# Three PSUM banks each for two kinds of scores, and a maximum taken bank by bank, in the narrow attention of a four-layer cross-attention kernel

## What is computed

```
cq = heads(ci @ cq_w, NH, CHD)                # NH = 16, CHD = 8
ckv = encoder_outputs @ ckv_w                 # 1601 rows of context
ck, cv = jnp.split(ckv, 2, axis=-1)
ck, cv = (heads(ck, NH, CHD), heads(cv, NH, CHD))
cctx = sdpa(cq, ck, cv, causal=False)         # softmax(q k / sqrt(8)) v
hidden_states = hidden_states + cctx @ cdense_w
```

## Time and profile before

| | us |
|---|---|
| median of 3 runs (5559.66 to 5569.71) | 5564.36 |
| the profiled execution's own time | 5575.49 |
| its span | 5573.7 |
| narrow attention in it, from the first to the last score (L1295, L1308) | 2295.7 to 3211.3 |
| mean granted TensorE clock over the span | 0.947 |

### The profile page before, as it was taken

The page is one execution under the profiler, slowest core; times in us unless marked ns, Lnnn a source line. Parts: engine busy times, 40 slices in busy tenths (PEclk is TensorE's granted clock), DMA queues, the critical chain, the costliest instruction groups (busy, mean ns, idle before and its releaser), DMA issues. The chain is left out here.

```text
span 5573.7 us, 95075 instructions
## 1 busy us (share of the span) xinstructions
PE 4920.9 (88%) x31384; PEld 3667.6 (66%) x31384; DVE 3625.5 (65%) x5212; ACT 3238.2 (58%) x4943; POOL 2589.8 (46%) x1723
## 2 busy tenths in 40 slices
PE   6999999999997799699899969767999999999987
PEld 5777676777766577455555559545777677667766
DVE  5777777777774344567666646235777777777764
ACT  5676767676662455355555620336677676767662
POOL 3666666676661233111111132003666676666661
PEclk9999999999998899699999979887999999999998
DMA  1000000000000000222222200101000000000000
GB/s 51 7 1 8 7 1 7 7 1 7 1 1 16 25 0 0 44 41 41 41 45 38 28 32 0 74 30 35 7 1 7 7 1 7 7 7 1 1 1 30
DMA packets 35067, 93.58 MB, mean 17 GB/s; under 512 B 12896, under 2 KB 22368, under 8 KB 33504
## 3 DMA queue, kind: packets, MB, share of 16 engines
q1 hardware_dynamic: 34656, 88.47, 7.2%
HBM read 55.80 MB, written 2.10 MB: 10 GB/s over the span
## 5 line engine op out<-in xcount | busy, mean ns | idle before, releaser
L1028 ACT ACTIVATE L_attn_probs<-L_attn_ps_s,L_attn_bias_now 128x512 f32<-128x512 f32 x1664 | 1093.8, 688 | 312.0 <-PE L_attn_ps_s L776 284.7
L739 POOL TENSOR_TENSOR L_attn_sums<-L_attn_sums,L_attn_probs 128x1024 f32<-128x1024 f32 x512 | 1224.7, 2392 | 103.8 <-POOL L_attn_sums L739 80.7
L930 DVE TENSOR_TENSOR L_attn_ps_x<-L_attn_probs,L_attn_ps_x 128x512 f32<-128x512 f32 x1408 | 978.0, 695 | 259.8 <-ACT L_attn_probs L1028 209.8
L942 DVE TENSOR_TENSOR L_attn_probs<-L_attn_probs,L_attn_ps_x 128x3072 f32<-128x3072 f32 (+2 forms) x384 | 933.7, 2460 | 85.9 <-PE L_attn_ps_x L825 85.9
L1034 ACT ACTIVATE L_attn_probs<-L_attn_probs 128x3072 f32<-128x3072 f32 (+2 forms) x384 | 774.7, 2051 | 122.9 <-DVE L_attn_probs L942 121.2
L774 PE MATMUL L_attn_ps_s<-L_attn_g_hi,L_attn_ctx_hi 128*128 128x512 f32 x1664 | 730.9, 439 | 125.6 <-ACT L_attn_probs L1028 93.0
L812 PE MATMUL L_attn_ps_u<-L_attn_probs,L_attn_v_sb 128*64 128x256 f32 (+1 forms) x6656 | 776.9, 384 | 0.0
L1564 ACT ACTIVATE L_cross_probsT<-L_cross_ps_st 128x512 f32<-128x512 f32 (+1 forms) x832 | 491.3, 597 | 367.9 <-PE L_cross_ps_st L1308 338.6
L775 PE MATMUL L_attn_ps_s<-L_attn_g_lo,L_attn_ctx_hi 128*128 128x512 f32 x1664 | 668.6, 402 | 0.0
L776 PE MATMUL L_attn_ps_s<-L_attn_g_hi,L_attn_ctx_lo 128*128 128x512 f32 x1664 | 667.0, 401 | 0.0
L1446 DVE TENSOR_REDUCE L_cross_part<-L_cross_ps_s 128x1 f32<-128x804 f32 x512 | 498.2, 992 | 242.5 <-PE L_cross_ps_s L1295 236.5
(11 more groups left out here) (288 smaller groups left out, 9218.4 us busy)
## 6 DMA issues: line engine op xcount, KB each, us to landing
L_cross_kx<-A SPq DMA_DIRECT2D x256, 100.5 KB, 2.8
L_attn_ctx_in<-in_ctxT SPq DMA_DIRECT2D x16, 804.0 KB, 4.4
memory_ctx<-in_ctx SPq DMA_DIRECT2D x8, 832.0 KB, 6.0
Bw<-in_ctxT SPq DMA_DIRECT2D x8, 804.0 KB, 4.4
memory_ctxT<-in_ctxT SPq DMA_DIRECT2D x8, 804.0 KB, 4.4
A<-in_L_mlp_w SPq DMA_DIRECT2D x4, 1024.0 KB, 6.0
X<-in_x SPq DMA_DIRECT2D x1, 2048.0 KB, 8.5
L_norm_wq<-in_L_w_wq SPq DMA_DIRECT2D x2, 1024.0 KB, 7.6
```

Source lines behind the costliest of these rows:

```text
L739: pool.tensor_tensor(both, both, p[:, k:k + 2, :], ALU.add).then_inc(added_up, 1)
L930: dve.tensor_tensor(high[:, :] if k == KT - 1 else ps_x[:, :], tile, ps_x[:, :], ALU.max).then_inc(maxed, 1)
L942: dve.tensor_tensor(s, s, ps_x[:, :].unsqueeze(1).to_broadcast([P, count, W]), ALU.subtract).then_inc(shifted, 1)
L1028: act.activation(probs[j % 2][:, k, :], ps_s[(KT * j + k) % 4][:, :], ACT.Identity, bias=bias_now[:, k:k + 1]).then_inc(taken, 1)
```

## The change

The 8 banks are divided in another way: three banks for the scores of the maximum, used in turn by single matmuls, and three for the turned scores. DVE takes the maximum of each bank by itself, so that there are 16 maxima of 402 columns in a slot where there were 8 of 804, and `join_tops` becomes a reduction over 4 numbers of each tile instead of a maximum of 2. Scores u (0 to 15) wait for the maximum that used their bank last, three before; turned scores k for the exponential three before. As 16 and 13 are not multiples of 3, the last of each goes into bank 1, so that u = 15, u = 1 of the next slot, k = 12 and k = 1 of the next slot wait for the use two before.

```
+    BANK_OF = [u % 3 for u in range(15)] + [1]
+    USED_BY = [max(v for v in range(u - 16, u) if BANK_OF[v % 16] == BANK_OF[u]) + 1 for u in range(16)]
+    ST_BANK = [k % 3 for k in range(KT - 1)] + [1]
+    ST_USED = [max(v for v in range(k - KT, k) if ST_BANK[v % KT] == ST_BANK[k]) + 1 for k in range(KT)]
...
-        part = ph.sb("part", [P, 2, 4, 2])
+        part = ph.sb("part", [P, 2, 4, 4])
...
-        ps_s = [ph.ps(f"ps_s{i}", [P, 2, BANK]) for i in range(2)]
-        ps_st = [ph.ps(f"ps_st{i}", [P, BANK]) for i in range(2)]
+        ps_s = [ph.ps(f"ps_s{i}", [P, BANK]) for i in range(3)]
+        ps_st = [ph.ps(f"ps_st{i}", [P, BANK]) for i in range(3)]
...
-            def half_scores(n, p, hh):
-                t, half = hh // 2, hh % 2
-                for c in range(2):
-                    k0 = (2 * half + c) * W
-                    ins = pe.matmul(ps_s[half][:, c, 0:W], qx[p % 4][0:ROWS, t * P:(t + 1) * P],
-                                    kx[p % 4][0:ROWS, k0:k0 + W], start=True, stop=True)
-                ins.then_inc(scored, 1)
+            def half_scores(n, p, hh, free):
+                for u in (2 * hh, 2 * hh + 1):
+                    t, c = u // 4, u % 4
+                    if free or u >= 3:
+                        pe.wait_ge(maxed, 16 * n + USED_BY[u])
+                    pe.matmul(ps_s[BANK_OF[u]][:, 0:W], qx[p % 4][0:ROWS, t * P:(t + 1) * P],
+                              kx[p % 4][0:ROWS, c * W:(c + 1) * W], start=True, stop=True).then_inc(scored, 1)
...
-                    if not (first and p == 0 and k < 2):
-                        pe.wait_ge(exped, KT * n + k - 1)
+                    if not (first and p == 0 and ST_USED[k] <= 0):
+                        pe.wait_ge(exped, KT * n + ST_USED[k])
...
             def half_max(n, p, hh):
-                t, half = hh // 2, hh % 2
-                dve.wait_ge(scored, 8 * n + hh + 1)
-                dve.sem_inc(dve_passed, 1)
-                dve.tensor_reduce(part[:, p % 2, t, half:half + 1], ps_s[half][:, :, 0:W], AXES_XY, ALU.max).then_inc(maxed, 1)
+                for u in (2 * hh, 2 * hh + 1):
+                    t, c = u // 4, u % 4
+                    dve.wait_ge(scored, 16 * n + u + 1)
+                    dve.sem_inc(dve_passed, 1)
+                    dve.tensor_reduce(part[:, p % 2, t, c:c + 1], ps_s[BANK_OF[u]][:, 0:W], AX_X, ALU.max).then_inc(maxed, 1)
...
-                dve.wait_ge(maxed, 8 * (n + 1))
+                dve.wait_ge(maxed, 16 * (n + 1))
...
-                dve.tensor_tensor(tops[p % 2][:, M0:M0 + 4], part[:, p % 2, :, 0], part[:, p % 2, :, 1], ALU.max).then_inc(tops_ready, 1)
+                dve.tensor_reduce(tops[p % 2][:, M0:M0 + 4], part[:, p % 2, :, :], AX_X, ALU.max).then_inc(tops_ready, 1)
```

More of the change, by code:

```diff
@@ L1307, in scores_turned @@
                 w = min(P, S - k * P)
-                pe.matmul(ps_st[(KT * p + k) % 2][0:w, :], kx[p % 4][0:M0 + 4, k * P:k * P + w], qx[p % 4][0:M0 + 4, :],
+                pe.matmul(ps_st[ST_BANK[k]][0:w, :], kx[p % 4][0:M0 + 4, k * P:k * P + w], qx[p % 4][0:M0 + 4, :],
                           start=True, stop=True).then_inc(st_made, 1)
@@ L1357, in slot @@
                         hh = HALF_AT[k]
-                        pe.wait_ge(maxed, 8 * (n + 2) + hh - 1)
-                        half_scores(n + 2, (p + 2) % NP, hh)
+                        half_scores(n + 2, (p + 2) % NP, hh, True)
                     if k == 2 and turning:
@@ L1431, in _ @@
                 for hh in range(8):
-                    if 8 * p + hh >= 2:
-                        pe.wait_ge(maxed, 8 * p + hh - 1)
-                    half_scores(p, p, hh)
+                    half_scores(p, p, hh, p > 0)
             pe.wait_ge(k_ready, 4)
@@ L1442, in half_max, with join_tops @@
             def half_max(n, p, hh):
-                t, half = hh // 2, hh % 2
-                dve.wait_ge(scored, 8 * n + hh + 1)
-                dve.sem_inc(dve_passed, 1)
-                dve.tensor_reduce(part[:, p % 2, t, half:half + 1], ps_s[half][:, :, 0:W], AXES_XY, ALU.max).then_inc(maxed, 1)
-            def join_tops(n, p):
-                dve.wait_ge(maxed, 8 * (n + 1))
-                dve.sem_inc(dve_passed, 1)
-                dve.tensor_tensor(tops[p % 2][:, M0:M0 + 4], part[:, p % 2, :, 0], part[:, p % 2, :, 1], ALU.max).then_inc(tops_ready, 1)
+                for u in (2 * hh, 2 * hh + 1):
[3 more added lines that the diff above has]
+                    dve.tensor_reduce(part[:, p % 2, t, c:c + 1], ps_s[BANK_OF[u]][:, 0:W], AX_X, ALU.max).then_inc(maxed, 1)
+            def join_tops(n, p):
+                dve.wait_ge(maxed, 16 * (n + 1))
+                dve.sem_inc(dve_passed, 1)
+                dve.tensor_reduce(tops[p % 2][:, M0:M0 + 4], part[:, p % 2, :, :], AX_X, ALU.max).then_inc(tops_ready, 1)
             def place_tops(n, p):
@@ L1563, in exponential @@
                 act.sem_inc(act_passed, 1)
-                act.activation(probsT[p % 2][0:w, k, :], ps_st[(KT * p + k) % 2][0:w, :], ACT.Exp, scale=SCALE).then_inc(exped, 1)
+                act.activation(probsT[p % 2][0:w, k, :], ps_st[ST_BANK[k]][0:w, :], ACT.Exp, scale=SCALE).then_inc(exped, 1)
             def take_u(J):
```

## The result

| | median us | against before, 95% interval |
|---|---|---|
| before (4 runs) | 5567.03 | |
| with the change (4 runs) | 5648.67 | 1.0148 (1.0130 to 1.0166), slower by 1.5% |

The change costs 82 us; the forecast was +44. The profiled execution took 5654.19, its span is 5652.2. The whole loss lies in the narrow attention: from the first turned maxima (`turn_tops`) to the last it takes 877.04 us before and 958.18 now.

A forecast was written before the change was run, and what follows sets the result against it. PE sets the pace, with PE and ACT waiting for each other; the change makes scores wait for DVE. Odd slots +45.6, even +1.4, first score passes +1.1, last slots -3.6: +44 us, 5609 predicted, own range 5580 to 5640.

The forecast's parts named there:

- Which way, and why: Narrow attention: PE's scores come to wait for DVE's maxima, waits for exponentials go, the kernel gets slower (chance 0.70).
- One sign: ACT in the narrow attention: exponentials would stand 0.49 us apart, where four behind each other stood 0.63 apart.
- the clock's rival: Last of three rivals: new waits lower PE's clock in each odd slot, 46 us more, 5655 us; chance 0.05.
- The odd slot: Scores wait for maxima behind DVE's other work: +0.80 and +0.72, +1.52 us a slot, 45.6 us over 30 slots.
- The even slot: p = 2 and 6: the third turned bank's gain is taken back by DVE, +0.09 us a slot, 1.4 us over 15.
- The price of a maximum: DVE, 402 columns: 0.574 us long and 0.49 apart, bounds 0.33 and 0.61.
- The 13 us more: DVE's maxima at the skill's 0.544 us a piece, with fixed cycles paid twice: the sum would be 13 us larger.
- The first rival: DVE doesn't decide; all waits for exponentials go, 22.5 pairs x 2.9 + 3.6 = 69 us, 5495 us; chance 0.15.
- The rule on banks: Rotating matmul groups through PSUM banks overlaps evacuation; by it the first rival would hold, borne out for ACT's side only.

The follow-up runs named there:

- Experiment 1: The change with four banks for the scores and two for the turned ones, the sixteen maxima kept: 5562.86 us, 0.9993 of the kernel before.
- experiment 2: The change with only DVE's order altered, place_tops behind half 3 (not in p = 4) and add behind half 6: 5574.12 us, 1.0020 of the kernel before.
- experiment 8: The change with useless turned-score matmuls in odd slots, three ahead of u = 7 and two ahead of u = 13: 5627.09 us, 1.0080 of the kernel before.
- Experiment 4: The change with each maximum over 201 of its 402 columns, the other half left out: 5540.38 us, 0.9950 of the kernel before.
- experiment 3: The change with the three banks of both kinds going round a whole batch, not one slot: 5644.19 us, 1.0136 of the kernel before.
- experiment 10: As experiment 9, but in p = 0 PE makes scores u = 2 and 3 behind the piece of V: 5546.82 us, 0.9976 of the kernel before.
- experiment 9: The change with banks going round the batch, DVE's place_tops and add later, odd slots' u = 7 and 13 behind V: 5570.93 us, 1.0016 of before.

## Why the prediction was right, and what it missed

- **Which way, and why: right.** PE's scores wait for DVE, exponentials no longer hold PE, maxima are 0.49 apart. Experiments 1 and 2 show it from two sides: a fourth bank, or DVE's other work put elsewhere, takes the loss away. One sign is only half there: exponentials are 0.49 apart where two lie ready (1.08 together), but four in the odd slot take 2.37, (2.37 - 0.60) / 3 = 0.59 apart, since ACT now waits for PE's scores instead:

```profile
2598.33 2.37 ACT L1566 ACTIVATE L_cross_probsT<-L_cross_ps_st 128x512 f32<-128x512 f32 x4 [0.63 <-PE L_cross_ps_st L1312]
```

- **The time: in part luck.** 5649 lies above the forecast's own range of 5580 to 5640, 40 us over its 5609. It lies 6 us from the 5655 of the clock's rival, whose mechanism is at work, but not in each odd slot and not at its price.
- **The odd slot: right in size in p = 3 and 7.** In p = 3 the first piece of V came 0.88 later (5.20 against 4.32) where +0.80 was forecast, the second 0.80 (3.86 against 3.06) where +0.72 was; the slot is 13.79, +1.67 for +1.52. p = 7 is 13.76 where it lies at 1.00 (experiment 8, first batch). But p = 1, counted with the same 1.52, lasts 13.83 for 12.73: +1.10.
- **The even slot: a little short.** 12.44, +0.30 where +0.09 stood: u = 1 delays the piece by 0.60 (0.49 forecast), and the next step wins 0.24 (0.35). The pair costs 1.97 instead of 1.61; over 22.5 pairs that would be 8 us more. p = 0 and 4, put at nothing, do grow: at 1.00 p = 0 of the last batch goes from 14.74 to 15.59, and p = 4 from 16.74 to 17.16 in experiment 8.
- **The price of a maximum: right.** 0.570 us measured, 0.574 taken. By the Trainium skill (VectorE: DVE Perf Modes, the section on the TRN2 errata) an estimate was 0.544; the trace stands 0.03 above it. The 13 us more that it gave the sum did not come, as maxima start 0.49 apart.
- **The clock: the term that was missing.** The step that failed is the last rival's "Against it: the waits of the clean pair leave 1.00, and the new ones are 0.6 to 1.5 us", with its chance of 0.05. The new waits do leave 1.00 in this p = 3, but in p = 4, 5 and 7 the kernel with the change is at 0.50 for longer than before (18, 30 and 28 us over all batches, of 83 counted to the end of the last slot; in p = 0, behind the loop's end, only 4). Time at 0.50 grew by 75 us, which can cost at most half of it, 37.5, where work takes twice as long. Experiment 8 gives a rate, 18.5 us for 53 fewer, 0.35 each: an estimate by it is 26 of the 82. With 44 and 8 that makes 78, and the account is no closer than that: p = 1 was counted too high, p = 0 and 4 too low, and the clock's share rests on one profiled execution of each kernel.
- **The first rival's price: wrong.** With 5495 it counted the 2.9 us a pair that the weight loads waited as PE's time. Experiment 4 takes over a third off DVE's maxima and reaches 5540, 1.0 a pair.
- **The rule on banks.** Experiment 1 against the change tells which scores need them: those for the maximum. The Trainium skill (Perfetto Trace Analysis, Matmuls) says to rotate matmul groups through banks so that evacuation overlaps. The traces agree for each side by itself, but there are eight banks to share: the third one for the turned scores took 38 us of idle time off PE, and the loss of the fourth for the maxima put 83 on it.

## What to carry to other kernels

Count banks by the longest stretch for which the engine that frees them is busy with something else, not by its mean load: DVE was idle a fifth of the time, and three banks were still too few wherever 0.7 us of other work stood among the maxima. If there is no bank to spare, move that work to where PE has a long step of its own. And price a new wait twice: as itself, and as the stretches at half the clock that it can bring elsewhere.

## What was not expected of the hardware

- Useless matmuls in PE's waits made a kernel faster: 5627 for 5649 us, 116 us at a granted clock of 0.50 in place of 168 (experiment 8).
- The same short waits left 1.00 in p = 3 and stood ahead of 0.50 in p = 7. It isn't bound to the slot: in experiment 3 p = 3 too had 3.4 us at 0.50 in six batches (15.35 instead of 13.77), behind a wait of 0.72. Why the one and not the other stays open.
- Where the hardware loop turns round, DVE starts 3.15 us late for nothing that the profile shows, and PE waits 2.93 us for it. It is no cost of the change alone: before it PE waited 2.56 us there, for an exponential. Other work put into that wait was worth 24 us, the clock's share included (experiment 10 against 9). DVE's timeline there with the change, and PE's before it:

```profile
2681.69 2.06 DVE L1448 TENSOR_REDUCE L_cross_part<-L_cross_ps_s 128x1 f32<-128x402 f32 x4 [3.15 <-issue]
...
2651.93 0.75 PE L1308 MATMUL L_cross_ps_st<-L_cross_qx,L_cross_kx 100*128 100x512 f32 x1 [2.56 <-ACT L_cross_probsT L1564]
```
